# Cross attention and a mixture of experts: eight dense experts replaced by sorted blocks of the two chosen ones

## The chip, the cores and the metric

One Trainium2 chip, one of its cores. The metric is the device time of one execution of the whole kernel, in microseconds (us). The engines are TensorE (PE, with PEld its weight load), VectorE (DVE), ScalarE (ACT), GpSimd (POOL) and SyncE (SP, which only issues transfers here). Each runs its own instructions in order and waits on counting semaphores for the others.

## What is computed

Everything is float32. `x` is 64 sequences of 128 rows of 256; `ctx` has 64 x 128 rows of 192. Cut to what matters:

```
q, (k, v) = layernorm(x) @ Wq, ctx @ Wkv             # 16 heads of 64
x = x + (softmax(q k^T / 8) v) @ Wproj + bproj
t = layernorm(x)                                     # 8192 rows of 256
p = softmax(t @ gate_w.T)                            # 8 experts
w, e = top_k(p, 2)
y = sum over the two chosen: w * silu(t @ expert_w[e].T + expert_b[e])
x = x + y @ combine_w.T
```

## The kernel before

**Precision.** A float32 operand of a product is split in a high part (`_hi`, written by ACT) and the rest (`_lo`, the source less the high part, written by DVE from the same PSUM bank; for two of them by POOL). A product is then three matmuls: hi*hi, hi*lo, lo*hi (`three`, `products`, L355 to L363).

**Tiling.** The unit is a *pair* of sequences, 256 rows, so there are 32 pairs. Inside a pair the loop goes over 8 *slots* `u`, one for each pair of heads. In slot `u` of pair `i` PE issues, in this order: `scores(i,u)` (6 matmuls of 256 columns in the one bank `s_ps`), `turn_probs(u-1)` (4 transposes), `queries_keys(u+2)` (11 matmuls of 256 columns), the general jobs marked mid, `project(u-2)` (6), `attend(u-1)` (6), the general jobs marked late. DVE takes the row maximum (`row_max`, L707, the first DVE instruction of a slot), the low parts, and the reciprocal of the sums (`inverse`, L713); ACT the four exponentials (L567) and the high parts; POOL multiplies the probabilities by the reciprocals (`normalise_probs`, L939), which `turn_probs` of the next slot waits for. The low part of those transposed probabilities goes through ACT and DVE before `attend`.

**General jobs.** A table written out by hand says in which slot each further piece of work is issued, and for which pair relative to `i`; the jobs rotate through three PSUM banks `gen_ps`, and a job waits until the bank's last job has been drained:

```python
JOBS = [
    (0, "mid", "combine", 0, -3),
    (0, "late", "expert", 3, -2),
    (1, "mid", "value", 2, 0),
    (1, "late", "expert", 4, -2),
    ...
    (7, "mid", "turn_mixed", 0, -2),
    (7, "late", "expert", 2, -1),
]
```

So each slot ends with one `expert` job: 6 matmuls of 512 columns, that is two experts on 128 rows, and a pair has 8 of them (all 8 experts on its 256 rows). All expert weights stay in SBUF, split (`wexp_s`).

**After an expert job.** DVE adds the bias out of PSUM (`expert_bias`, L741), ACT takes tanh (L592) and adds one (L596), POOL multiplies (`silu`, L946), multiplies by the routing weights (L957, L960) and adds to the sum (`mix`, L962, L966), all on 128x512. Routing weights (`route_top`, `route_weights`, DVE, slot 6 of the next pair) are zero for the six experts not chosen. `turn_mixed` and `combine` (4 transposes, 12 matmuls of 256 columns) follow once a pair; the result plus `x1` goes out. In the last slots, where there is no attention left, DVE does what POOL does elsewhere (L748, L757, L763).

The matmuls of a job, and POOL's part behind it (`c` is the job's number within 128 rows):

```python
                for a in range(2):
                    terms += three(x1T[par], wexp_s, lambda y: y[:, a, t * P:(t + 1) * P],
                                   lambda w: w[:, a, c * 512:(c + 1) * 512])
                return products(bank[:, :], terms)
...
                pool.tensor_tensor(weighted.rearrange("p (e c) -> p e c", e=2), src, w, ALU.mult).then_inc(mix_done, 1)
                pool.wait_ge(mix_done, nth(j, 8, k))
                pool.tensor_tensor(acc, acc, weighted, ALU.add).then_inc(mix_step, 1)
```

**Order of the program.** `steps` writes pairs -1 to 3 and the last ones out, and runs pairs 4 to 28 in a loop of two pairs (`Fori`, 13 rounds). Once a pair POOL also computes two reciprocal roots for the norms (`rsqrt`, L932 and L934; the one for the next pair's norm in slot 1, ahead of `normalise_probs` of that slot), and adds the projection bias (L973). SP has two loads and one store a pair.

Of the kernel before, what the change touches and what calls it, by code (L numbers as in the profile page):

```python
# [5 lines left out]
P = 128  # L6
F32 = mybir.dt.float32
F32R = mybir.dt.float32r
U32 = mybir.dt.uint32
ALU = mybir.AluOpType  # L10
ACT = mybir.ActivationFunctionType
AX_X = mybir.AxisListType.X

# [4 lines left out]
EPS = 1e-5  # L28

JOBS = [
    (0, "mid", "combine", 0, -3),
    (0, "late", "expert", 3, -2),
    (1, "mid", "value", 2, 0),
    (1, "late", "expert", 4, -2),
    (2, "mid", "value", 3, 0),
    (2, "late", "expert", 5, -2),
    (3, "mid", "turn_x1", 0, -1),
    (3, "late", "expert", 6, -2),  # L40
    (4, "mid", "gate", 0, -1),
    (4, "mid", "turn_x", 0, 1),
    (4, "late", "expert", 7, -2),
    (5, "mid", "turn_gate", 0, -1),
    (5, "mid", "value", 0, 1),
    (5, "late", "expert", 0, -1),
    (6, "mid", "value", 1, 1),
    (6, "late", "expert", 1, -1),
    (7, "mid", "turn_mixed", 0, -2),
    (7, "late", "expert", 2, -1),  # L50
]
BANKS = 3
PER_PAIR = {"expert": 8, "value": 4, "turn_x": 1, "turn_x1": 1, "gate": 1, "turn_gate": 1,
            "turn_mixed": 1, "combine": 1}


def plus(j, n):
    return j + n if n else j


def nth(j, per, k):

    return plus(j * per if per != 1 else j, k + 1)


def exists(j, pairs):
    return not isinstance(j, int) or 0 <= j < pairs


def wait(eng, sem, count):  # L70

    if not isinstance(count, int) or count > 0:
        eng.wait_ge(sem, count)


def steps(eng, pairs, step):


    for i in (-1, 0, 1, 2, 3):
        step(i, i % 2)  # L80
    with eng.Fori(4, pairs - 3, 2) as i:
        step(i, 0)
        step(i + 1, 1)
    for i in (pairs - 2, pairs - 1, pairs, pairs + 1, pairs + 2):
        step(i, i % 2)


def xattn_moe_kernel(nc, x, ctxT, wq, wkv, wkv_rest, wproj, bproj, gateT, expertT, expert_b, combineT, out):
# [4 lines left out]
    N2 = 2 * P  # L93

    x_pairs = x.rearrange("(j t p) c -> j p t c", t=2, p=P)
    out_pairs = out.rearrange("(j t p) c -> j p t c", t=2, p=P)

    with ExitStack() as stack:
# [9 lines left out]

# [4 lines left out]
        wexp_s = hilo("wexp_s", [P, 2, E * C])  # L113
# [3 lines left out]
        ebias = sb("ebias", [P, E * C])  # L117
        pbias = sb("pbias", [P, C])
        ident = sb("ident", [P, P])
        minus_half = sb("minus_half", [P, 2])  # L120
        eps = sb("eps", [P, 2])
        expert_no = sb("expert_no", [P, E])

# [4 lines left out]


# [3 lines left out]

# [89 lines left out]
        def bank_free(pe, i, n):  # L223

            m = n
            while True:
# [7 lines left out]
                if isinstance(i, int) and i - step_back < -1:  # L234
                    return

        def tail_no(j, k):

# [807 lines left out]
```

## Time and profile before

| | |
|---|---|
| time, 3 runs | 1789.58 us median (1788.9 to 1792.51) |
| span of the profiled execution | 1787.3 us (its own time beyond the span is not listed; the median is 2.3 us above it) |
| first and last slot's row maximum | 29.5 us, 1726.5 us |
| PE busy | 1665.2 us (93%) |
| DVE busy | 1541.9 us (86%) |
| ACT busy | 1385.2 us (78%) |
| POOL busy | 1256.7 us (70%) |
| bytes moved by DMA | 42.89 MB |
| granted TensorE clock | 1.00 up to 1700 us, then 0.89, 0.84 and 0.80 in the three last stretches of some 30 us |

Times count from the start of the span. Busy times of an engine are merged, so overlapping instructions count once; a matmul's own duration contains its latency, and the distance between the starts of two of them is what one costs. The distance between two row maxima is the length of a slot.

### The profile page before, as it was taken

The page shows a single profiled execution, that of the slowest core. Times are in us where ns is not written, and L with a number is a line of the kernel's source. Part 1 is how long each engine was busy: PE and PEld are TensorE (multiplying, and loading weights), DVE is VectorE, ACT ScalarE, POOL GpSimd, SP SyncE. Part 2 cuts the span into 40 slices and gives each one's busy share as a digit, 9 for nine tenths or more (in the row PEclk, how much of TensorE's full clock was granted, in tenths as well). Part 3 has the DMA queues.
Part 4 walks back from the last instruction along what each step waited for, and adds up shares of the span by engine and source line. Part 5 has one row for each costly group of instructions (what it writes and reads, how often), then busy time and mean ns, then how long its engine had stood idle before and what let it go on. Part 6 is the DMA issues. An engine that isn't in the chain of part 4 may idle for free.

```text
span 1787.3 us, 39425 instructions
## 1 busy us (share of the span) xinstructions
PE 1665.2 (93%) x11584; PEld 1529.9 (86%) x11584; DVE 1541.9 (86%) x3569; ACT 1385.2 (78%) x4484; POOL 1256.7 (70%) x1235
## 2 busy tenths in 40 slices
PE   5999999999999999999999999999999999999986
PEld 4899889888888888888888898888898888888974
DVE  6888988888988888888888988889888888988877
ACT  6987878777878778788787887778787787887862
POOL 3557777777777777777776777777777777777760
PEclk9999999999999999999999999999999999999997
DMA  5000000000000000000000000000000000000000
GB/s 197 25 19 19 19 25 25 16 22 19 18 24 25 12 25 18 18 24 24 13 24 13 24 24 25 12 19 18 24 25 12 25 18 19 24 24 13 13 7 12
DMA packets 33609, 42.89 MB, mean 24 GB/s; under 512 B 2464, under 2 KB 28448, under 8 KB 32800
## 3 DMA queue, kind: packets, MB, share of 16 engines
q1 hardware_dynamic: 33440, 41.30, 7.2%
q14 instruction: 145, 1.19, 0.2%
q8 instruction: 24, 0.39, 0.1%
HBM read 32.91 MB, written 8.39 MB: 23 GB/s over the span
## 4 chain that ended last, share of the span: by engine, by line
PE 68%; DVE 16%; issue 12%; ACT 3%; DMA 1%; DVEq 1%; POOL 0%; SPq 0%; ACTq 0%; POOLq 0%
PE gen_ps L357 26%; PE qk_ps L357 11%; PE proj_ps L357 9%; PE o_ps L357 8%; PE s_ps L357 8%; DVE o_s_lo L675 4%; PE pT_ps L396 4%; DVE k_s_lo L675 2%; ACT probs L567 1%; DVE scratch L695 1%; DVE scratch L741 1%; DVE neg_max L707 1%; PE gen_ps L439 1%; DVE v_s_lo L675 1%; DVE top_atf L802 1%
## 5 line engine op out<-in xcount | busy, mean ns | idle before, releaser
L939 POOL TENSOR_TENSOR probs<-probs,inv_sums 128x512 f32<-128x512 f32 x256 | 268.8, 1050 | 275.6 <-DVE inv_sums L713 273.6
L946 POOL TENSOR_TENSOR scratch<-scratch 128x512 f32<-128x512 f32 x244 | 313.7, 1286 | 129.5 <-ACT scratch L596 129.5
L567 ACT ACTIVATE probs<-s_ps,neg_max 128x128 f32<-128x128 f32 x1024 | 363.2, 372 | 48.7 <-DVE neg_max L707 47.1
L552 ACT CAST pT_s_hi<-pT_ps 128x512 fp32r<-128x512 f32 x256 | 150.5, 588 | 223.6 <-PE pT_ps L396 220.7
L707 DVE TENSOR_REDUCE neg_max<-s_ps 128x4 f32<-128x512 f32 x256 | 175.9, 687 | 130.0 <-PE s_ps L357 100.7
L962 POOL TENSOR_TENSOR scratch<-scratch 128x512 f32<-128x512 f32 x183 | 236.8, 1294 | 14.3
L592 ACT ACTIVATE scratch<-scratch 128x512 f32<-128x512 f32 x256 | 161.9, 633 | 84.4 <-DVE scratch L741 79.2
L675 DVE TENSOR_TENSOR o_s_lo<-o_ps,o_s_hi 64x256 fp32r<-64x256 f32 x512 | 213.5, 417 | 5.6 <-ACT o_s_hi L552 1.9
L675 DVE TENSOR_TENSOR k_s_lo<-qk_ps,k_s_hi 64x256 fp32r<-64x256 f32 x512 | 213.3, 417 | 3.5
L567 ACT ACTIVATION_READ_ACCUMULATOR probs<-s_ps,neg_max 128x1 f32 x1024 | 215.7, 211 | 0.0
L357 PE MATMUL gen_ps<-wexp_s_hi,x1T_hi 128*128 128x512 f32 x512 | 205.5, 401 | 3.5 <-DVE scratch L741 3.4
L960 POOL TENSOR_TENSOR scratch<-scratch,route_w 128x512 f32<-128x512 f32 x183 | 190.4, 1040 | 26.0 <-POOL scratch L946 21.8
L357 PE MATMUL gen_ps<-wexp_s_lo,x1T_hi 128*128 128x512 f32 x512 | 204.5, 399 | 0.0
L357 PE MATMUL gen_ps<-wexp_s_hi,x1T_lo 128*128 128x512 f32 x512 | 203.4, 397 | 0.0
L552 ACT CAST k_s_hi<-qk_ps 64x256 fp32r<-64x256 f32 x512 | 190.9, 373 | 3.0
L552 ACT CAST o_s_hi<-o_ps 64x256 fp32r<-64x256 f32 x512 | 185.1, 361 | 5.3 <-PE o_ps L357 1.3
L357 PE MATMUL o_ps<-pT_s_hi,v_s_hi 128*128 128x256 f32 x512 | 148.1, 289 | 37.7 <-DVE pT_s_lo L675 37.7
L675 DVE TENSOR_TENSOR pT_s_lo<-pT_ps,pT_s_hi 128x512 fp32r<-128x512 f32 x256 | 176.8, 691 | 6.5
L357 PE MATMUL proj_ps<-wproj_s_hi,o_s_hi 128*128 128x256 f32 x512 | 155.3, 303 | 27.7 <-DVE o_s_lo L675 26.1
L741 DVE TENSOR_TENSOR scratch<-gen_ps,ebias 128x512 f32<-128x512 f32 x256 | 174.4, 681 | 3.1 <-PE gen_ps L357 3.0
L357 PE MATMUL qk_ps<-xT_hi,wq_s_hi 128*128 128x256 f32 x512 | 166.0, 324 | 3.9 <-DVE k_s_lo L675 3.8
L596 ACT ACTIVATE scratch<-scratch 128x512 f32<-128x512 f32 x244 | 154.8, 635 | 1.1
(134 smaller groups left out, 5640.3 us busy)
## 6 DMA issues: line engine op xcount, KB each, us to landing
x_raw<-in_x SPq DMA_DIRECT2D x32, 256.0 KB, 2.9
c_raw<-in_ctxT SPq DMA_DIRECT2D x32, 256.0 KB, 2.7
later<-in_x SPq DMA_DIRECT2D x32, 256.0 KB, 2.7
out_dram<-later SPq DMA_DIRECT2D x32, 256.0 KB, 2.2
scratch<-in_expertT SPq DMA_DIRECT2D x2, 1024.0 KB, 6.7
scratch<-in_wq SPq DMA_DIRECT2D x1, 1024.0 KB, 7.3
scratch<-in_wkv SPq DMA_DIRECT2D x1, 1024.0 KB, 9.3
ebias<-in_wkv_rest SPq DMA_DIRECT2D x1, 1024.0 KB, 11.4
```

The source lines that it names most:

```text
L357: mm = pe.matmul(out_ap, l, r, start=start and n == 0, stop=stop and n == len(terms) - 1, skip_group_check=skip)
L552: last = act.copy(to, of)
L567: last = act.activation(probs[p % 2][:, k, :], s_ps[:, k * P:(k + 1) * P], ACT.Exp, bias=neg_max[p % 2][:, k:k + 1], accum_out=sums[p % 2] ...
L592: act.activation(th[k % 2], z[k % 2], ACT.Tanh, scale=0.5).then_inc(tanh_done, 1)
L596: act.activation(th[k % 2], th[k % 2], ACT.Copy, bias=1.0).then_inc(tanh_plus, 1)
L675: last = dve.tensor_tensor(lo, of, hi.bitcast(F32), ALU.subtract)
L707: dve.tensor_reduce(neg_max[p % 2][:, :], s_ps[:, :].rearrange("p (k n) -> p k n", k=4), AX_X, ALU.max, negate=True).then_inc(max_done, 1)
L741: dve.tensor_tensor(z[k % 2], gen_ps[b][:, :], ebias[:, c * 512:(c + 1) * 512], ALU.add).then_inc(drained["expert"], 1)
L939: pool.tensor_tensor(probs[b][:, :, :], probs[b][:, :, :], inv_sums[b][:, :].unsqueeze(2).broadcast_to([P, 4, P]), ALU.mult).then_inc(prob ...
L946: pool.tensor_tensor(th[k % 2], th[k % 2], z[k % 2], ALU.mult).then_inc(silu_done, 1)
L960: pool.tensor_tensor(weighted.rearrange("p (e c) -> p e c", e=2), src, w, ALU.mult).then_inc(mix_done, 1)
L962: pool.tensor_tensor(acc, acc, weighted, ALU.add).then_inc(mix_step, 1)
```

## The change

The eight dense experts go. Each row is computed for its two experts only:

* **Routing** (DVE, PE): the two chosen experts of a row become a 0/1 mark (`hot`); one small PE job (`rank`, slot 7 of the next pair) counts how many earlier rows chose the same expert, and `route_rows` turns that into row numbers of a DRAM table `sorted_x`, which has a region for each expert.
* **Scatter** (POOL): in slot 0, two pairs later, 4 indirect transfers of 128 rows each write the normalised rows to `sorted_x`.
* **Chunks:** the 32 pairs are cut in chunks of 10, 9, 8 and 5. At a chunk's end `list_blocks` (DVE, some 25 small instructions) rounds each expert's count up to 128 and lists the blocks; `clear` (POOL, 8 indirect transfers) fills the rest of the last blocks with zeros. A chunk has 4n+7 blocks: 47, 43, 39 and 27, or 156.
* **Blocks:** one a slot. SP reads row and expert number from SBUF into a register and loads 128 rows (128 KB), the expert's split weights out of a DRAM table (512 KB) and its bias. PE transposes the rows (2 transposes), multiplies (6 matmuls of 256 columns and one for the bias); ACT and DVE split the rows and do tanh and (tanh+1)*z on 128x256; SP stores the block to `sorted_y`. The buffers form a ring of three.
* **Gather** (POOL): once a chunk's blocks are stored, each of its pairs takes two slots: 4 indirect transfers fetch the rows (128 KB each), POOL multiplies by the weights (128x1024) and adds (128x512), then `turn_mixed` and `combine` as before. `x1` of each pair is stored to DRAM and loaded back.
* **Program:** written out in full, with no loop. By the plan, chunk 0's blocks are turned in slots 92 to 138, chunk 1's in 164 to 206, chunk 2's in 228 to 266, chunk 3's in 268 to 294; gathers are at every second slot from 143, 211, 271 and 299. Attention ends with slot 255, the program with slot 313.

The core of the diff:

```diff
-JOBS = [
...
-def steps(eng, pairs, step):
...
+CHUNKS = (10, 9, 8, 5)
+RING = 3
...
+        for c, end in enumerate(self.ends):
+            at = max(at, SLOTS * (end + 1) + 4)
+            for b in range(self.blocks[c]):
+                self.turn[at] = (c, b, self.first[c] + b)
+                at += 1
+            free = max(free, at + 4)
+            for m in range(end - CHUNKS[c], end):
+                self.gather[free] = m
+                free += 2
...
+            def load_block(c, b, n):
...
+                if b == 0:
+                    sp.wait_ge(cleared, 16 * E * (c + 1))
...
+                wait(sp, made["turn_block"], n - RING + 1)
+                row = sp.value_load(blocks[b:b + 1, c, 0:1], min_val=0, max_val=ROWS - P)
+                sp.dma_start(x_block[r], sorted_x[bass.ds(row, P), :]).then_inc(x_block_in[r], 16)
+                wait(sp, made["expert"], n - RING + 1)
+                e = sp.value_load(blocks[b:b + 1, c, 1:2], min_val=0, max_val=E)
+                sp.dma_start(w_block[r][:, :, :].bitcast(F32).rearrange("p a n -> p (a n)"),
+                             expert_table[bass.ds(e * P, P), :]).then_inc(w_block_in[r], 16)
+                sp.dma_start(b_block[r][0:2, :].bitcast(F32),
+                             bias_table[bass.ds(e * 2, 2), :]).then_inc(b_block_in[r], 16)
+
+            def store_block(c, b, n):
+                sp.wait_ge(drained["expert"], n + 1)
+                sp.dma_start(sorted_y[c][b * P:(b + 1) * P, :], y_block[n % RING]).then_inc(y_stored[n % RING], 16)
...
+                if s - 2 in plan.turn:
+                    store_block(*plan.turn[s - 2])
+                if s + 2 in plan.turn:
+                    load_block(*plan.turn[s + 2])
...
+            def expert(n, bank):
+                pe.wait_ge(drained["turn_block"], n + 1)
+                pe.wait_ge(w_block_in[n % RING], 16 * (n // RING + 1))
...
+                for a in range(2):
+                    terms += three(xs, (w[:, a, :], w[:, 2 + a, :]), lambda y: y[:, a, :], lambda part: part)
+                terms.append((ones_s[:, :], b_block[n % RING][:, :]))
+                return products(bank[:, 0:C], terms)
...
+            def expert_out(n):
+                dve.wait_ge(tanh_done, n + 1)
+                wait(dve, y_stored[n % RING], 16 * (n // RING))
+                bank = gen_ps[plan.bank("expert", n)]
+                dve.scalar_tensor_tensor(out=y_block[n % RING], in0=th[n % 2], scalar=1.0, in1=bank[:, 0:C],
+                                         op0=ALU.add, op1=ALU.mult).then_inc(drained["expert"], 1)
...
+            def scatter(j):
+                pool.wait_ge(xn2_done, j + 1)
+                pool.wait_ge(rows_done, j + 1)
+                for k in range(4):
+                    pool.indirect_dma_start(
+                        out=sorted_x, out_offset=bass.IndirectOffsetOnAxis(ap=row_of[:, j % 4, k:k + 1], axis=0),
+                        in_=xn2[j % 2][:, k // 2, :], in_offset=None).then_inc(scattered[j % 2], 16)
+
+            def clear(c):
+                pool.wait_ge(clear_ready, c + 1)
+                pool.wait_ge(zero_ready, 1)
+                wait(pool, cleared, 16 * E * c)
+                for e in range(E):
+                    pool.indirect_dma_start(
+                        out=sorted_x, out_offset=bass.IndirectOffsetOnAxis(ap=clear_at[:, c, e:e + 1], axis=0),
+                        in_=zero_rows[:, :], in_offset=None).then_inc(cleared, 16)
+
+            def gather(m):
...
+                for r in range(RING):
+                    pool.wait_ge(y_stored[r], 16 * blocks_in_ring(r, through))
+                pool.wait_ge(y_rows_done, c + 1)
+                wait(pool, mixed_done, m - 1)
+                for k in range(4):
+                    pool.indirect_dma_start(
+                        out=got[m % 2][:, k, :], out_offset=None, in_=sorted_y[c],
+                        in_offset=bass.IndirectOffsetOnAxis(ap=y_row_of[:, m, k:k + 1], axis=0)).then_inc(
+                            gathered[m % 2], 16)
+
+            def mix(m):
+                pool.wait_ge(gathered[m % 2], 64 * (m // 2 + 1))
+                pool.wait_ge(top_w_done, m + 1)
+                y = got[m % 2]
+                pool.tensor_tensor(y, y, top_w[:, m, :].unsqueeze(2).broadcast_to([P, 4, C]),
+                                   ALU.mult).then_inc(weighted, 1)
+                pool.wait_ge(weighted, m + 1)
+                wait(pool, made["turn_mixed"], m - 1)
+                pool.tensor_tensor(mixed[m % 2], y[:, 0:4:2, :], y[:, 1:4:2, :], ALU.add).then_inc(mixed_done, 1)
...
+            for s, i, u in slots():
+                now, before, nxt = exists(i), exists(i - 1), exists(i + 1)
+                if u == 1 and nxt:
+                    rsqrt(i + 1, 0)
+                if now:
+                    normalise_probs(i, u)
+                if u == 2 and before:
+                    rsqrt(i - 1, 1)
+                if s - 2 in plan.gather:
+                    mix(plan.gather[s - 2])
+                if s in plan.gather:
+                    gather(plan.gather[s])
+                if u == 0 and exists(i - 2):
+                    scatter(i - 2)
+                    if i - 1 in plan.ends:
+                        clear(plan.ends.index(i - 1))
```

## Rows read from the trace of the kernel before

**Rows 1.** The page, busy time of each engine.

```profile
PE 1665.2 (93%) x11584; PEld 1529.9 (86%) x11584; DVE 1541.9 (86%) x3569; ACT 1385.2 (78%) x4484; POOL 1256.7 (70%) x1235
```

**Rows 2.** The page, chain that ended last, shares of the span by engine.

```profile
PE 68%; DVE 16%; issue 12%; ACT 3%; DMA 1%; DVEq 1%; POOL 0%; SPq 0%; ACTq 0%; POOLq 0%
```

**Rows 3.** Windows: length, busy time (x count) of each engine, clock, DMA share, GB/s.

```profile
68.00:95.00 27.00, 25.92 (x198) 23.91 (x197) 24.88 (x61) 22.54 (x78) 10.29 (x12) 1.00 0.10 31
```

**Rows 4.** Timeline, DVE row maxima: start, duration, idle before and releaser.

```profile
29.48 0.69 DVE L707 TENSOR_REDUCE neg_max<-s_ps 128x4 f32<-128x512 f32 x1
...
68.22 0.69 DVE L707 TENSOR_REDUCE neg_max<-s_ps 128x4 f32<-128x512 f32 x1
...
112.45 0.69 DVE L707 TENSOR_REDUCE neg_max<-s_ps 128x4 f32<-128x512 f32 x1 [0.86 <-PE s_ps L357]
...
164.27 0.69 DVE L707 TENSOR_REDUCE neg_max<-s_ps 128x4 f32<-128x512 f32 x1 [0.36 <-PE s_ps L357]
...
217.43 0.69 DVE L707 TENSOR_REDUCE neg_max<-s_ps 128x4 f32<-128x512 f32 x1 [0.46 <-PE s_ps L357]
...
976.78 0.69 DVE L707 TENSOR_REDUCE neg_max<-s_ps 128x4 f32<-128x512 f32 x1 [2.38 <-issue]
...
1726.47 0.69 DVE L707 TENSOR_REDUCE neg_max<-s_ps 128x4 f32<-128x512 f32 x1 [2.27 <-PE s_ps L357]
```

**Rows 5.** Timeline, PE: starts of neighbouring matmuls and four transposes.

```profile
1000.37 0.28 PE L357 MATMUL s_ps<-k_s_hi,q_s_hi 128*128 128x256 f32 x1
...
1000.49 0.28 PE L357 MATMUL s_ps<-k_s_lo,q_s_hi 128*128 128x256 f32 x1
...
1005.18 0.39 PE L357 MATMUL gen_ps<-wexp_s_hi,x1T_hi 128*128 128x512 f32 x1
...
1005.41 0.39 PE L357 MATMUL gen_ps<-wexp_s_lo,x1T_hi 128*128 128x512 f32 x1
```

**Rows 6.** Groups by line and shape: count, busy us, mean ns, idle before.

```profile
L946 POOL TENSOR_TENSOR scratch<-scratch 128x512 f32<-128x512 f32 x244 | 313.7, 1286 | 129.5 <-ACT scratch L596 129.5
L939 POOL TENSOR_TENSOR probs<-probs,inv_sums 128x512 f32<-128x512 f32 x256 | 268.8, 1050 | 275.6 <-DVE inv_sums L713 273.6
...
L741 DVE TENSOR_TENSOR scratch<-gen_ps,ebias 128x512 f32<-128x512 f32 x256 | 174.4, 681 | 3.1 <-PE gen_ps L357 3.0
...
L675 DVE TENSOR_TENSOR q_s_lo<-qk_ps,q_s_hi 128x256 fp32r<-128x256 f32 x256 | 104.5, 408 | 44.4 <-ACT k_s_hi L552 44.4
...
L934 POOL TENSOR_TENSOR rstd<-var_eps,minus_half 128x2 f32<-128x2 f32 x64 | 44.8, 700 | 5.0
...
L819 DVE TENSOR_TENSOR route_w<-chosen 128x16 f32<-128x16 f32 x32 | 35.9, 1121 | 3.4
...
L1010 POOL TENSOR_SCALAR_AFFINE_SELECT ident<-ident 128x128 f32<-128x128 f32 x1 | 0.3, 292 | 0.2 <-POOL ident L1008 0.2
```

**Rows 7.** Timeline of pair 1, POOL multiplications and the transposes after one.

```profile
71.48 1.04 POOL L939 TENSOR_TENSOR probs<-probs,inv_sums 128x512 f32<-128x512 f32 x1 [1.65 <-DVE inv_sums L713]
...
75.61 1.04 POOL L939 TENSOR_TENSOR probs<-probs,inv_sums 128x512 f32<-128x512 f32 x1 [0.26 <-DVE inv_sums L713]
...
77.68 0.60 PE L396 MATMUL pT_ps<-ident,probs 128*128 128x128 f32 x4
```

**Rows 8.** Timeline of SP: start and length of an issue.

```profile
1.76 0.43 SPq L321 DMA_DIRECT2D scratch<-in_wq  x1
...
3.69 5.76 SPq L327 DMA_DIRECT2D gate_raw<-in_gateT  x1
```

**Rows 9.** DMA issues: count, KB each, median us from issue to landing.

```profile
x_raw<-in_x SPq DMA_DIRECT2D x32, 256.0 KB, 2.9
...
out_dram<-later SPq DMA_DIRECT2D x32, 256.0 KB, 2.2
```

**Rows 10.** Timeline, DVE: gate logits of the last pair.

```profile
1753.42 0.25 DVE L779 TENSOR_REDUCE logits<-gen_ps 128x8 f32<-128x16 f32 x2
```

**Rows 11.** The chain that ended last, its last transposes.

```profile
1778.20 1.10 PE gen_ps L439 x4
```

More of the change, by code:

```diff
@@ L28 @@
 EPS = 1e-5
-JOBS = [
[L33 to L51, printed above, removed]
@@ L52 @@
-BANKS = 3
[L53 to L67, printed above, removed]
+ROUND = 8388608.0
+CHUNKS = (10, 9, 8, 5)
+RING = 3
+BANKS = 3
+ATTENTION_JOBS = {
+    1: [("value", 2, 0)],
+    2: [("value", 3, 0)],
+    3: [("turn_x1", 0, -1)],
+    4: [("gate", 0, -1), ("turn_x", 0, 1)],
+    5: [("turn_gate", 0, -1), ("value", 0, 1)],
+    6: [("value", 1, 1)],
+    7: [("rank", 0, -1)],
+}
@@ L353, in _ @@
+                if s - 5 in plan.gather:
+                    m = plan.gather[s - 5]
+                    sp.wait_ge(drained["combine"], m + 1)
+                    sp.dma_start(out_pairs[m], outb[m % 2].rearrange("p (t c) -> p t c", t=2)).then_inc(
+                        out_stored[m % 2], 16)
+            for b in range(2):
+                sp.wait_ge(out_stored[b], 16 * (pairs // 2))
         @block.tensor
@@ L504, in general @@
                     else:
[L505 removed]
+                        mm = combine(n, bank)
                     mm.then_inc(made[kind], 1)
[L508 to L532 removed]
@@ L534, in _ @@
-            steps(pe, pairs, step)
-        def previous_expert(i, u, back=1):
-            for slot, _, kind, k, off in JOBS:
-                if kind == "expert" and slot == (u - back) % SLOTS:
-                    off -= u < back
-                    if exists(plus(i, off), pairs):
-                        return k, plus(i, off), off
-            return None
+            pe.wait_ge(const_b, 2)
+            for s, i, u in slots():
+                now, before, nxt = exists(i), exists(i - 1), exists(i + 1)
+                if now:
+                    scores(i, u)
+                if u == 0 and before:
+                    turn_probs(i - 1, 7)
+                if u > 0 and now:
+                    turn_probs(i, u - 1)
+                if u < 6 and now:
+                    queries_keys(i, u + 2)
+                if u >= 6 and nxt:
+                    queries_keys(i + 1, u - 6)
+                general(s, "mid")
+                if u < 2 and before:
+                    project(i - 1, 6 + u)
+                if u >= 2 and now:
+                    project(i, u - 2)
+                if u == 0 and before:
+                    attend(i - 1, 7)
+                if u > 0 and now:
+                    attend(i, u - 1)
+                general(s, "late")
```

1132 lines of the change are left out of this document (622 added, 510 removed).

## The prediction, made before any run of the changed kernel

> **What bounds the kernel now.** I read the page's busy line first: PE 93%, DVE 86%, ACT 78%, POOL 70% [rows 1]. Two engines are near full, so the chain that ended last decides between them: 68% of it is PE and 16% DVE [rows 2]. The issue share, 12%, has to be found elsewhere: it sits at the loop.
>
> Then the starts of the row maxima, one a slot [rows 4]. They cut the span in a start (29.5 us), 255 slots (1697 us) and an end of 61 us. Pair 3 takes 217.43 - 164.27 = 53.2 us. Pair 1 is a natural experiment: its slots 0 to 4 have no expert at all, only three expert jobs fall in it, and it takes 112.45 - 68.22 = 44.2 us. In its window without experts PE is busy 25.9 of 27 us and DVE 24.9 [rows 3], so attention alone keeps both nearly full. POOL is not: 10.3 us.
>
> **What an expert job costs today.** Let A be a pair without experts and e one job. Pair 1 is A + 3e. Pair 3 is A + 8e + 3.4, where 3.4 is 1.9 for `turn_mixed` and `combine` (16 PE instructions at about 0.12, the distance of two starts [rows 5]) and an estimate of 1.5 for DVE instructions that take longer beside POOL (the group of 16 elements that averages 1121 ns [rows 6] is the plainest). So 53.2 - 3.4 - 44.2 = 5e: e = 1.1, A = 40.9. A job costs 6 x 0.23 = 1.4 us of PE [rows 5] and 0.68 of DVE [rows 6]; a fifth of the PE time is hidden.
>
> **Removed.** 8e a pair; the three POOL instructions of 128x512 a job; all tanh work on 512 columns; the loop. At a back edge DVE's row maximum shows 2.38 us of issue idle [rows 4]; with 12 back edges, and about a half given back in the next slot, that is 15 to 28 us. The sum below has it, since it is built from unrolled pairs.
>
> **Added, attention part (slots 0 to 255).**
> - Routing: `rank`, five row instructions, two `hot`: some 8 DVE instructions of 0.13 us (two in 0.25 [rows 10]). 1.1 us a pair, so a pair is 42.0.
> - Base: 29.5 + 32 x 42.0 - 3 (pair 0 took 38.7, 68.22 - 29.48) - 5 (the last slot's own length) = 1366.
> - Blocks: 118 of the 156 fall in attention slots. One is 7 x 0.12 + 2 transposes of 0.12, 1.1 us of PE, and two DVE instructions of 128x256, 0.41 each [rows 6]. By PE's ratio to a dense job that is 0.85 us of slot, by DVE's 1.3; unhidden, 1.9. I take 0.85, since PE holds the chain: 100. Their ACT work (two instructions of 256 columns) replaces two of 512.
> - 19 pairs combined here: 19 x 1.9 = 36. Three block lists of some 25 linked small instructions, 0.2 each: 15.
>
> Without the indirect transfers slot 255 would start at 1517, 210 us earlier than today.
>
> **The indirect transfers** decide. POOL must write the descriptors of 128 rows; the trace of before has none. Call one c. From below: a small POOL instruction, 0.29 [rows 6]. From above: SP's issue of the gate weights, many small pieces, 5.76 us, against 0.43 for a plain one [rows 8]. Nearest in kind are POOL instructions that go over 128 rows: 1.05 and 1.29 [rows 6]. I take 1.1.
>
> What is late next: `normalise_probs` of the following slot stands behind them on POOL, `turn_probs` on PE waits for it, and all of PE's slot stands behind that. In pair 1 two of these POOL instructions start 4.13 us apart (slots 0 and 1), and after the second `turn_probs` starts 77.68 - 76.65 = 1.0 us after its end [rows 7]; that is the slack.
> - Scatter in slot 0: 4c = 4.4, plus `rsqrt` 0.9 (0.70 [rows 6] and a smaller one) and the multiplication 1.05, is 6.35. Late by 2.2, less 1.0 slack: 1.2 x 30 pairs = 36.
> - Clear, 8c = 8.8 behind a scatter, three times in attention: 26.
> - A gather slot has mix of the pair before (2 x 1.05 + 1.29 = 3.4), 4.4 and 1.05, 8.85 us, against a slot of 5.3 and 1.0 slack: 2.5 x 19 = 48.
>
> Slot 255 then starts at 1366 + 100 + 36 + 15 + 36 + 26 + 48 = 1627.
>
> **The tail, from there.** Attention's last pair needs 26.9 us to its gate logits today [rows 4, 10], and about 2 more to its row numbers: 29. Scatter to 33.4, meanwhile the list to about 34, clear 8.8, landing 2.2 (a store [rows 9]): 45. SP then reads the row number and loads, 2.9 [rows 9], turned and multiplied at about 50. Eleven blocks of chunk 2 fit in before. Chunk 3's 27 blocks go at about 3 us each (four SP issues of 0.43 [rows 8], two register reads that no row shows, a round trip of DVE between). POOL in that time gathers 8 pairs, and each is 4.4, 2.2 landing, 3.4 mix, one after the other since mix precedes the next gather: 10.0, so from 45 to 125, longer than PE's 19 blocks (107); seven more blocks, 146; last out and stored, 150. Then five pairs at 10.0 with nothing beside them, 200. The end, from the turned mix to the end of the span, is 1787.3 - 1778.2 = 9.1 today [rows 11]. Tail: 209 us, against 61.
>
> Sum: 1627 + 209 = **1836 us**, against the span of 1787.3. The median stands 2.3 above its span; I write 1836, as the sum is not that fine. The expert work saved is given back once in POOL's queue and once in a tail.
>
> **A rule weighed.** The row of 16 elements with a mean of 1121 ns [rows 6] shows DVE held up while POOL works. The Trainium skill, "SBUF — State Buffer", Who interferes with whom, says the two share a port pair by an exclusive lock, and that descriptor generation on GpSimd is shut out while DVE copies in its two-port mode: the first half helps this change (by that, DVE gets its 1.5 us a pair back, which the sum has), the second speaks against it and is rival 2. The skill's "DMA: Bandwidth & Descriptors", Anatomy of one DMA, gives about 2.0 us fixed for a transfer issued from GpSimd, mostly completion; with that for the landing the sum would be some 3 us less.
>
> **Rivals.**
> 1. Descriptors are cheap, c = 0.7 or less (nearer to a small POOL instruction). Then scatter hides (4.75 against 5.13), clear costs 16, gathers 16, slot 255 starts at 1549, the tail is 185: 1734 us, faster. It decides below c = 0.92, where scatter costs 12, clear 21, gathers 31 and the tail about 197. For: POOL is idle 17 of 27 us in pair 1. Against: no POOL instruction over 128 rows is below 1.05. Chance 0.26.
> 2. A descriptor waits for DVE: with one DVE instruction of 0.4 [rows 6] in front of each transfer, c = 1.5: 85 + 36 + 77 and a tail of 233: 1948. For: DVE is busy 24.9 of 27 us, though few of its instructions are copies. Chance 0.14.
> 3. SP becomes the bound: registers and four issues at over 5 us a block. In attention hidden by the slot; in the tail 38 blocks at 5 instead of 3, less what POOL's pace covers: 1880 to 1900. Chance 0.10.
> 4. Blocks hide nothing: 1.9 instead of 0.85 on 118, 1960. Against: dense jobs hid a fifth. Chance 0.04.
> The forecast, c between 0.92 and 1.4: 0.46, with 1790 to 1920 as its own range.
>
> **Chances and range.** Within 0.2% of 1789.6 is about what a measurement can tell from no change; the forecast's low edge and rival 1's upper edge meet there: 0.03. Faster 0.26, slower 0.71. Range: down to 1734 for rival 1, up to 1950 for rivals 2 and 3.
>
> **What would show it.** The profile after should have: PE near 75 to 80% busy and POOL's queue issue rows of about 1.1 us in fours; `turn_probs` waiting for POOL in slots 1 and in gather slots, hundreds of waits of 1 to 3 us; pairs without blocks and gathers (3 to 9) of 43 us; 7 us more for each pair with a block in every slot; the last row maximum at about 1627; some 200 us after it with PE mostly idle, and in the last 50 only POOL's gathers and mixes. Wrong would make it: c off 1.1 by a few tenths, each 0.1 being about 26 us; blocks at another price than 0.85; a wait for `w_block` or for SP that I don't see.

## The result and the profile after

The changed kernel takes 2006.9 us (median of 4 runs, 2004.5 to 2011.6) where the one before takes 1790.7 us in the same comparison: ratio 1.1215, 95% interval 1.1197 to 1.1232. It is slower, as I forecast, but by 216 us where I had 46, and 57 us above the top of my range. The profiled execution's span is 2009.8 us.

The page after, busy time; it answers to [rows 1]:

```profile
PE 1596.0 (79%) x11516; PEld 1471.5 (73%) x11516; DVE 1436.0 (71%) x3879; ACT 1202.7 (60%) x4298; POOL 795.4 (40%) x865
```

Every engine has less to do than before, and none is full. So this is a kernel that waits, and the view to read is the chain's local form, the waits. (The chain that ended last has only 4% of the span attributed here, and says nothing.) Who waited for whom: total, times, longest.

```profile
POOL probs L1087 <- DVE inv_sums L821: 991.2, 209, 9.9
ACT pT_s_hi L637 <- PE pT_ps L481: 385.6, 244, 12.1
DVE stage L844 <- ACT stage L694: 180.4, 148, 1.8
PEld pT_ps L481 <- POOL probs L1087: 139.2, 102, 11.0
```

POOL's 991 us cost nothing by themselves: it has little to do, and waits for its next job. The third row is the one that I had not priced. `expert_out` (L844), DVE's last instruction on a block, waits 148 times, 1.2 us each, for ACT's tanh (L694), and DVE is an engine on which all else stands behind it.

Two stretches show the size. The row maxima (L814), one a slot, as in [rows 4]; first those of a pair without blocks (its start, the two ends of its slot 2, the next pair's start), then those of a pair with a block in every slot (its start, its slots 2 to 4, the next pair's start):

```profile
382.39 0.69 DVE L814 TENSOR_REDUCE neg_max<-s_ps 128x4 f32<-128x512 f32 x1
...
392.10 0.68 DVE L814 TENSOR_REDUCE neg_max<-s_ps 128x4 f32<-128x512 f32 x1
399.16 0.68 DVE L814 TENSOR_REDUCE neg_max<-s_ps 128x4 f32<-128x512 f32 x1
...
426.95 0.69 DVE L814 TENSOR_REDUCE neg_max<-s_ps 128x4 f32<-128x512 f32 x1
...
699.66 0.68 DVE L814 TENSOR_REDUCE neg_max<-s_ps 128x4 f32<-128x512 f32 x1
...
712.29 0.68 DVE L814 TENSOR_REDUCE neg_max<-s_ps 128x4 f32<-128x512 f32 x1
720.26 0.68 DVE L814 TENSOR_REDUCE neg_max<-s_ps 128x4 f32<-128x512 f32 x1
728.26 0.68 DVE L814 TENSOR_REDUCE neg_max<-s_ps 128x4 f32<-128x512 f32 x1
...
757.71 0.68 DVE L814 TENSOR_REDUCE neg_max<-s_ps 128x4 f32<-128x512 f32 x1
```

The pair with blocks takes 757.71 - 699.66 = 58.05 us. The one without takes 426.95 - 382.39 = 44.56 (the slot shown, 7.06 us, has the scatter stall in it). The difference is 13.5 us over eight blocks: **1.69 us a block**, where I had 0.85. And here is why, in the slot from 720.26: ACT, DVE, POOL and PE in order of time.

```profile
720.98 0.37 ACT L665 ACTIVATE probs<-s_ps,neg_max 128x128 f32<-128x128 f32 x1 [0.38 <-DVE neg_max L814]
...
722.36 0.63 ACT L657 CAST cT_hi<-c_raw 128x512 fp32r<-128x512 f32 x1
722.38 0.69 DVE L772 TENSOR_TENSOR pT_s_lo<-pT_ps,pT_s_hi 128x512 fp32r<-128x512 f32 x1
722.87 0.39 ACT L637 CAST q_s_hi<-qk_ps 128x256 fp32r<-128x256 f32 x1
723.14 0.76 ACT L637 CAST k_s_hi<-qk_ps 64x256 fp32r<-64x256 f32 x2
723.92 0.38 ACT L694 ACTIVATE stage<-gen_ps 128x256 f32<-128x256 f32 x1
...
724.34 0.42 DVE L844 SCALAR_TENSOR_TENSOR stage<-stage,gen_ps 128x256 f32<-128x256 f32 x1 [1.26 <-ACT stage L694]
...
724.67 0.17 DVE L821 RECIPROCAL inv_sums<-sums 128x4 f32<-128x4 f32 x1
724.81 0.50 PE L444 MATMUL gen_ps<-w_block,xbT_hi 128*128 128x256 f32 x2 [0.70 <-DVE stage L844]
724.92 1.12 POOL L1087 TENSOR_TENSOR probs<-probs,inv_sums 128x512 f32<-128x512 f32 x1 [4.79 <-DVE inv_sums L821]
```

The softmax sums are there when ACT's last exponential ends, near 722.5. DVE could take the reciprocal (L821) at 723.1, when the low part of pT is done. It does so at 724.67, because `expert_out` stands ahead of it and waits for a tanh that ACT has placed behind the exponentials and the high parts of q and k.

Three things stand behind that wait. One is the reciprocal, with POOL's multiplication and PE's `turn_probs` after it. One is the rest of DVE's slot: from 724.34 to the next row maximum at 728.26 DVE is never idle, so the 1.26 us are in the slot's length. And one is a PSUM bank: `expert_out` is also what empties it, and PE waits 0.70 us for that (724.81) ahead of the next block's matmuls, with the next slot's scores behind them. `turn_probs` then goes at 726.46, right behind those scores and 0.4 us after POOL has finished.

Over the three pairs from 699.66 to 873.83 us, DVE is idle 12.7 us a pair, 10.9 of them at `expert_out`. PE waits 5.3 us a pair for the bank that `expert_out` empties, and 2.2 us for POOL's probabilities; in the pairs without blocks that last wait is 2.1 us. So what the late tanh adds on PE is the wait for the bank, and not the path over the reciprocal.

An indirect transfer, the other open price, is nearly uniform. POOL in the tail: four gathers of a pair and its multiplication and addition, first beside the blocks of the last chunk, then (second group) with nothing beside them:

```profile
1835.80 0.98 POOL L1124 DMA_INDIRECT stage<-sorted_y,y_row_of  x1 [0.15 <-POOL stage L1137]
...
1840.48 0.95 POOL L1124 DMA_INDIRECT stage<-sorted_y,y_row_of  x1 [0.31 <-issue]
1846.08 1.89 POOL L1133 TENSOR_TENSOR stage<-stage,top_w 128x1024 f32<-128x1024 f32 x1 [4.65 <-DMA stage<-sorted_y,y_row_of]
1848.05 1.26 POOL L1137 TENSOR_TENSOR stage<-stage 128x512 f32<-128x512 f32 x1
1849.46 0.98 POOL L1124 DMA_INDIRECT stage<-sorted_y,y_row_of  x1
...
1963.56 0.95 POOL L1124 DMA_INDIRECT stage<-sorted_y,y_row_of  x1 [0.30 <-issue]
1964.81 0.94 POOL L1124 DMA_INDIRECT stage<-sorted_y,y_row_of  x1 [0.30 <-issue]
1967.63 1.89 POOL L1133 TENSOR_TENSOR stage<-stage,top_w 128x1024 f32<-128x1024 f32 x1 [1.87 <-DMA stage<-sorted_y,y_row_of]
```

0.95 us and 0.30 between two: c = 1.26 from start to start, where I had 1.1. Beside blocks the gathered rows land 4.65 us after the last issue's end and a pair takes up to 13.7 us (1849.46 - 1835.80); alone, 1.87 us, and a pair takes 9.96 (mean of the last four steps).

### The profile page after: what moved, and what is told of

Its sections match the earlier page's. It is cut to its first block and busy times, and to the rows that moved or that the text cites. A ratio compares the mean times of both kernels' runs of the same rounds, so it can differ in the third digit from the quotient of the medians.

```text
span 2009.8 us, 39286 instructions
## 1 busy us (share of the span) xinstructions
PE 1596.0 (79%) x11516; PEld 1471.5 (73%) x11516; DVE 1436.0 (71%) x3879; ACT 1202.7 (60%) x4298; POOL 795.4 (40%) x865
## 5 line engine op out<-in xcount | busy, mean ns | idle before, releaser
L481 PE MATMUL pT_ps<-ident,probs 128*128 128x128 f32 x1024 | 162.9, 283 | 118.5 <-POOL probs L1087 118.2
L814 DVE TENSOR_REDUCE neg_max<-s_ps 128x4 f32<-128x512 f32 x256 | 175.2, 684 | 60.8 <-PE s_ps L444 60.2
L481 PEld LDWEIGHTS pT_ps<-ident,probs 128*128 128x128 f32 x1024 | 116.5, 143 | 139.2 <-POOL probs L1087 139.2
L844 DVE SCALAR_TENSOR_TENSOR stage<-stage,gen_ps 128x256 f32<-128x256 f32 x156 | 65.6, 421 | 180.4 <-ACT stage L694 180.4
L444 PE MATMUL proj_ps<-wproj_s_hi,o_s_hi 128*128 128x256 f32 x512 | 165.2, 323 | 33.2 <-DVE o_s_lo L772 31.0
L444 PE MATMUL gen_ps<-w_block,xbT_hi 128*128 128x256 f32 x624 | 145.9, 328 | 28.0 <-DVE stage L844 22.5
L1124 POOL DMA_INDIRECT stage<-sorted_y,y_row_of x128 | 123.9, 968 | 75.4 <-issue 71.3
L444 PE MATMUL o_ps<-pT_s_hi,v_s_lo 128*128 128x256 f32 x512 | 147.4, 288 | 0.0
L444 PE MATMUL o_ps<-pT_s_lo,v_s_hi 128*128 128x256 f32 x512 | 147.3, 288 | 0.0
L444 PE MATMUL s_ps<-k_s_hi,q_s_hi 128*128 128x256 f32 x512 | 146.4, 286 | 0.8 <-ACT probs L665 0.8
L1103 POOL DMA_INDIRECT sorted_x<-xn,row_of x128 | 126.4, 987 | 51.4 <-issue 34.3
```

The costliest lines, as they stand in the source:

```text
L444: mm = pe.matmul(out_ap, l, r, start=start and n == 0, stop=stop and n == len(terms) - 1, skip_group_check=skip)
L481: mm = pe.transpose(pT_ps[:, k * P:(k + 1) * P], probs[p % 2][:, k, :], ident[:, :])
L814: dve.tensor_reduce(neg_max[p % 2][:, :], s_ps[:, :].rearrange("p (k n) -> p k n", k=4), AX_X, ALU.max, negate=True).then_inc(max_done, 1)
L844: dve.scalar_tensor_tensor(out=y_block[n % RING], in0=th[n % 2], scalar=1.0, in1=bank[:, 0:C], op0=ALU.add, op1=ALU.mult).then_inc(drained ...
L1103: pool.indirect_dma_start(out=sorted_x, out_offset=bass.IndirectOffsetOnAxis(ap=row_of[:, j % 4, k:k + 1], axis=0), in_=xn2[j % 2][:, k // ...
L1124: pool.indirect_dma_start(out=got[m % 2][:, k, :], out_offset=None, in_=sorted_y[c], in_offset=bass.IndirectOffsetOnAxis(ap=y_row_of[:, m, ...
```

## The experiments

Ten kernels, in three groups (the first four, the next four, the last two), each with its own runs of the kernel before on the same chip: 1789.5, 1782.8 and 1785.8 us. All ratios are to those; between groups the ratios are what compares, and spans of the traces within one percent.

**The loop by itself.** The dense kernel with its loop written out, all else as before:

```diff
-    for i in (-1, 0, 1, 2, 3):
-        step(i, i % 2)
-    with eng.Fori(4, pairs - 3, 2) as i:
-        step(i, 0)
-        step(i + 1, 1)
-    for i in (pairs - 2, pairs - 1, pairs, pairs + 1, pairs + 2):
+    for i in range(-1, pairs + 3):
         step(i, i % 2)
```

> The dense kernel with its loop over pairs written out, nothing else changed. If the back edges cost what the trace of before shows (the pairs inside the loop take 52.1 and 56.2 us in turn, 54.15 on average, the written-out ones 53.1), 26 pairs save about 1.05 us each: 1790 - 27 = 1763 us. If the written-out program pays for fetching instructions instead, no change or slower.

Measured: 1762.4 us, ratio 0.9844 (0.9827 to 0.9860). The loop cost 27 us, inside my 15 to 28. So one part of the change is a gain, and the sparse part alone costs 245 us, not 216.

**Who holds the block slots.** Two kernels part the two orders. In the first, DVE's `expert_out` goes behind the reciprocal and the low parts of q and k, so that nothing in the softmax waits for tanh:

```diff
-                if s - 2 in plan.turn:
-                    expert_out(plan.turn[s - 2][2])
...
                 if u >= 6 and nxt:
                     qk(i + 1, u - 6)
+                if s - 2 in plan.turn:
+                    expert_out(plan.turn[s - 2][2])
```

> The changed kernel; DVE issues expert_out after inverse and after the low parts of q and k, instead of before inverse. Theory A (DVE waits for a tanh that ACT runs behind the high parts of q and k, 1.2 us a block, and holds up inverse and so the loop over the probabilities): a slot with a block falls from 7.26 us to about 6.4, 118 slots, so some 100 us less, about 1905. Theory B (the three PSUM banks: the next block's transposes wait for expert_out): the later issue makes it longer, 2007 to 2060. Theory C (PE or DVE full): same.

In the second, ACT does the tanh of a block ahead of the exponentials; DVE's order is unchanged:

```diff
+                if s - 2 in plan.turn:
+                    tanh(plan.turn[s - 2][2])
                 if now:
                     exps(i, u)
...
-                if s - 2 in plan.turn:
-                    tanh(plan.turn[s - 2][2])
```

> The changed kernel; ACT issues the block's tanh before the exponentials of the slot, instead of behind the high parts of q and k. Theory A: DVE's wait goes, the exponentials start 0.3 us later; 118 slots save 0.6 to 0.9 us: 1900 to 1935. Theory B: the bank is free earlier too, so this gains more than the late expert_out: below 1905. Theory C: same.

The first was slower than the changed kernel itself: 2044.1 us, ratio 1.1412 (1.1378 to 1.1446). Its block pairs take 59.5 to 62.5 us. Waits for the bank, first of the whole changed kernel, then of this one:

```profile
PE gen_ps L552 <- DVE stage L844: 48.8, 26, 2.5
...
PE gen_ps L444 <- DVE stage L844: 22.5, 31, 1.0
```

```profile
PEld gen_ps L444 <- DVE stage L844: 101.4, 73, 2.3
...
PE gen_ps L444 <- DVE stage L844: 86.5, 72, 2.1
```

`expert_out` frees the PSUM bank of the block, and PE, in order too, stands before the next job that wants that bank. In its pairs from 703.40 to 886.92 us the reciprocal comes 2.9 us after the row maximum on average, as in a pair without blocks, and PE never waits for POOL's probabilities; but it waits 10.2 us a pair for the bank, where the changed kernel has 5.3. An early reciprocal alone gains nothing.

The second was far faster: 1896.5 us, ratio 1.0598 (1.0581 to 1.0616), 110 us off the changed kernel. Its block pairs take 50.74 us against 44.56: **0.77 us a block**. Two neighbouring pair starts, then a stretch of a slot in its trace (slot 7 of its pair; the one shown above was slot 3):

```profile
681.81 0.68 DVE L814 TENSOR_REDUCE neg_max<-s_ps 128x4 f32<-128x512 f32 x1
...
732.55 0.68 DVE L814 TENSOR_REDUCE neg_max<-s_ps 128x4 f32<-128x512 f32 x1
```

```profile
676.76 0.39 ACT L694 ACTIVATE stage<-gen_ps 128x256 f32<-128x256 f32 x1
...
677.03 0.37 ACT L665 ACTIVATE probs<-s_ps,neg_max 128x128 f32<-128x128 f32 x1
...
677.64 0.69 DVE L772 TENSOR_TENSOR pT_s_lo<-pT_ps,pT_s_hi 128x512 fp32r<-128x512 f32 x1
...
678.25 0.41 DVE L844 SCALAR_TENSOR_TENSOR stage<-stage,gen_ps 128x256 f32<-128x256 f32 x1
...
678.58 0.18 DVE L821 RECIPROCAL inv_sums<-sums 128x4 f32<-128x4 f32 x1
678.84 1.04 POOL L1087 TENSOR_TENSOR probs<-probs,inv_sums 128x512 f32<-128x512 f32 x1 [4.16 <-DVE inv_sums L821]
```

`expert_out` follows the low part of pT with no wait, and the reciprocal comes 2.4 us after the slot's row maximum (676.17), where the changed kernel's slot 7 has 3.9. In such pairs DVE is idle 4.7 us instead of 12.7, and PE waits 1.0 us for the bank instead of 5.3. The block's own work is cheap, and was priced right; the place of one ACT instruction doubled it. Both times fell where my expectations had put theory B, the bank (2007 to 2060, and below 1905): theory A, the reciprocal, had the first at 1905.

**The scatter.** One transfer in each of the slots 0 to 3 instead of four in slot 0 (at a chunk's end still all four):

```diff
-                if u == 0 and exists(i - 2):
+                if u < 4 and exists(i - 2) and i - 1 not in plan.ends:
+                    scatter(i - 2, (u,))
+                if u == 0 and i - 1 in plan.ends:
                     scatter(i - 2)
...
```

> The changed kernel; a pair's four scatter transfers are issued one each in slots 0 to 3 instead of all in slot 0 (not in the four steps in which a clear follows). If the 1.6 us by which slot 2's start is late (7.06 against 5.48 us) is POOL's queue: 26 pairs x 1.6 = 42 us less, 1965. If it were the transfers themselves (SBUF or DMA), no change.

Measured: 1981.2 us, ratio 1.1077 (1.1058 to 1.1095), 26 us off, where I expected 42. Pairs without blocks fall from 44.56 to 43.22. Most block pairs stay at 57.9 to 58.2: the slot that held the scatter stall takes 7.05 us instead of 7.98, but two slots later one takes 9.0 instead of 8.07. Why it gives the gain back was not traced.

**The gather's order on POOL.** The gather of a pair ahead of the mix of the pair before:

```diff
-                if s - 2 in plan.gather:
-                    mix(plan.gather[s - 2])
                 if s in plan.gather:
                     gather(plan.gather[s])
+                if s - 2 in plan.gather:
+                    mix(plan.gather[s - 2])
```

> The changed kernel; in a slot POOL issues the next pair's four gathers ahead of the mix of the pair before. In the tail one pair takes POOL 12.5 us beside block loads (four transfers 5.1, landing 4 to 5 waited out, mix 3.3) and 10.0 without. Theory: the landing is waited out only because mix stands right behind the transfers; swapped, a pair is 8.4 us, so the last five pairs save 5 x 1.6 = 8 us, and the eight before them save 8 x 4 = 32 us of POOL, of which some is then PE's or SP's block pace: 1975 to 1990. Rival: the tail goes at the pace of the blocks, not of POOL: only the 8 us, 2000. In the attention part no change (the mix comes two slots later).

A miss: I expected 1975 to 1990, and no change in attention. In the tail it does what was meant (a pair every 8.8 us; the tail is 216 us instead of 245), but the kernel took 2024.8 us, ratio 1.1365 (1.1348 to 1.1383), where the changed kernel has 1.1215. The last row maximum comes at 1803.0 instead of 1765.2: the gather pairs in attention rise from 57.5 and 65.3 us to 65.3 and 75.9. Waits of its pairs with gathers, 1000 to 1080 us:

```profile
PE gen_ps L524 <- POOL stage L1137: 13.7, 4, 4.0
```

The mix now comes 5 us later in its slot, and PE's `turn_mixed`, which stands ahead of attention's own work, waits 4.0 us for it. In that stretch of the changed kernel this row is absent; PE waits there for POOL's `probs` instead (16.6 us in 4 waits).

**The weights.** The experts' weights and biases are loaded for the first three blocks only and those are used for all (that part of the computation is left out, and PE waits for those first loads only):

```diff
             def load_block(c, b, n):
...
+                if n >= RING:
+                    return
```

> The changed kernel with the expert weights and biases of a block loaded for the first three blocks only; every later block is multiplied by whatever the ring holds, so the output is of other experts. It takes 153 x 514 KB of loads and SP's second wait away and leaves all else. Theory: in the attention part the loads cost nothing (each has some three slots), so the block pairs stay at 58.0 us; in the tail the landing of a gather falls from 4.5 to 2 us, so POOL's cycle falls from 12.5 to 10 and the tail by 20 to 30 us: 1980. Rival: SP's queue and the loads are part of the block slots' length: block pairs shorter, 1900 to 1950.

Measured: 1983.4 us, ratio 1.1123 (1.1106 to 1.1140); the span is 1983.2 us, against 2009.8. The last row maximum is at 1765.9, as with the loads: 512 KB a block cost attention nothing. The tail is 217 us instead of 245. Windows over the tail's first part, of the changed kernel, then of this one (length, busy time and count of PE, PEld, DVE, ACT, POOL, clock, DMA share, GB/s):

```profile
1800.00:1930.00 130.00, 65.65 (x351) 61.15 (x352) 31.41 (x66) 23.20 (x58) 63.90 (x57) 0.70 0.73 226
```

```profile
1800.00:1900.00 100.00, 54.37 (x302) 50.90 (x303) 26.93 (x56) 20.25 (x50) 58.02 (x52) 0.74 0.48 142
```

**All of it spread.** Tanh first, the scatter spread, the clear two transfers a slot over slots 0 to 3 (the first three chunks' blocks then start two slots later):

> The changed kernel with the tanh before the exponentials, one scatter transfer a slot, and the clears of the first three chunks two a slot over slots 0 to 3 (their blocks start two slots later); not the last chunk's. From 1896 for the tanh alone: 26 for the scatter as measured, and the three clears cost 10.8 us each in slot 2: with three transfers a slot, 3.8 us, they fit into POOL's idle 3.3 to 4.7 us and the 1.0 us of slack, so 25 to 32 less: about 1840. If the clears' cost is SP held at its wait for them, it stays: 1870.

```diff
-                if u == 0 and exists(i - 2):
-                    scatter(i - 2)
+                if i - 1 == pairs:
+                    if u == 0:
+                        scatter(i - 2)
+                        clear(len(CHUNKS) - 1)
+                elif u < 4 and exists(i - 2):
+                    scatter(i - 2, (u,))
                     if i - 1 in plan.ends:
-                        clear(plan.ends.index(i - 1))
+                        clear(plan.ends.index(i - 1), (2 * u, 2 * u + 1))
```

Measured: 1861.5 us, ratio 1.0439 (1.0419 to 1.0459), where I expected 1840; block pairs 50.15 us. The first pair with a clear takes 46.5 us instead of 60.6, but two of its block slots have moved to the next pair as well; its slots 0 to 3, ahead of any block's matmuls, take 24.0 us instead of 34.7. Then the same with each pair's four gathers two a slot over two slots, the multiplication in the third and the addition in the fourth, `turn_mixed` and `combine` a slot later:

```diff
+                if s in plan.gather:
+                    gather(plan.gather[s], (0, 1))
+                if s - 1 in plan.gather:
+                    gather(plan.gather[s - 1], (2, 3))
                 if s - 2 in plan.gather:
                     mix(plan.gather[s - 2])
-                if s in plan.gather:
-                    gather(plan.gather[s])
...
+                if s - 3 in plan.gather:
+                    add_two(plan.gather[s - 3])
```

> As the run before, and the gathers spread too: two transfers a slot over two slots, the multiplication in the third, the addition in the fourth, gathers ahead of them; turn_mixed and combine one slot later. In the attention part a gather costs 3.2 to 3.7 us now, of which 1.9 is PE's own work: 19 x 1.5 = 28 less. In the tail POOL's pair falls from 12.5 and 10.0 to 8.4: 40 less. From 1840: about 1775, 14 under the dense kernel. Rival: the tail is at the blocks' pace: 1800.

Measured: 1811.0 us, ratio 1.0157 (1.0143 to 1.0171), the last row maximum at 1594.4 and a tail of 217 us. I expected 1775: attention gave 20 us instead of 28, the tail 27 instead of 40. The first pair full of gathers takes 49.0 us, where the run before has 56.0, and the next 60.3 instead of 63.9 (5.1 of each a block list); in that next pair PE's wait for POOL's probabilities is down from 9.9 to 0.9 us, so the slots hardly queue on POOL any more.

**Against the tail.** The last kernel with chunks of 12, 10, 6 and 4 pairs, so that less is left at the end:

```diff
-CHUNKS = (10, 9, 8, 5)
+CHUNKS = (12, 10, 6, 4)
```

> The kernel with tanh first and all indirect transfers spread, with its chunks changed from 10, 9, 8 and 5 pairs to 12, 10, 6 and 4, so that the last chunk has 23 blocks instead of 27 and 10 gathered pairs fall behind the last row maximum instead of 13. Theory that the tail is set by the stored blocks of the last chunk (they were waited for until about 164 us behind the last row maximum): 36 blocks instead of 40 in the tail at 4.1 us each end 16 us earlier, and 4 pairs of 8.7 us follow instead of 5: the tail falls from 217 to about 192 us. The attention part takes 4 more blocks at 0.77 and 3 more gathered pairs at about 2 us, so +9: near 1795 us, level with the dense kernel (ratio 1.00). Rival, that GpSimd's mixing of the earlier chunk sets the tail and the blocks wait on nothing: 3 pairs fewer at 8.7, which the attention part gives back in part: 1790 to 1800 too, but with GpSimd not idle ahead of the last chunk's gathers. If the blocks are bound by their loads beside the gathers, the tail falls by less than 10 us and the kernel stays near 1810.

And the same with the tail's additions on DVE:

```diff
+                if s - 3 in plan.gather and s > SLOTS * (pairs + 1):
...
+                    dve.tensor_tensor(mixed[m % 2], y[:, 0:4:2, :], y[:, 1:4:2, :], ALU.add).then_inc(mixed_done, 1)
```

> The same chunks of 12, 10, 6 and 4, and behind the last row maximum the addition of the two weighted rows goes from GpSimd to VectorE. If GpSimd's cycle of four transfers, a product and an addition (8.7 us) sets the end, it falls to about 7.2 us, and the four last pairs end 6 us earlier: about 1789 us. If the stored blocks set the end, only those four pairs gain, and the middle of the tail stays: the same 6 us. If VectorE in order holds the addition behind a block's output, nothing is gained or up to 10 us lost.

Measured: 1801.8 us, ratio 1.0091 (1.0076 to 1.0107), and 1800.2 us, ratio 1.0089 (1.0075 to 1.0103). Both gains are smaller than expected (1795 and 1789), the second nothing that can be told. With fewer blocks left (36 instead of 40), the last chunk's gathers still start 165 us after the last row maximum (164 in the kernel before it). Its waits and the window over 1680 to 1720 show why:

```profile
ACT xbT_hi L637 <- PE gen_ps L552: 20.1, 9, 4.3
PE gen_ps L552 <- DMA stage<-sorted_x: 13.6, 7, 4.0
...
1680.00:1720.00 40.00, 26.09 (x142) 23.93 (x142) 13.20 (x27) 9.92 (x24) 31.64 (x27) 0.66 0.93 298
```

PE's transposes of a block wait for its rows, up to 4.0 us, with the DMA engines 93% busy at 298 GB/s. That looks like the third outcome that I had written down for this run, blocks bound by their loads. But SP, which issues these loads, hardly waits either: 0.9 us in these 40. It issues the rows of ten blocks there, and over the last chunk never two of them less than 3.26 us apart; each block is four issues of some 0.3 us and two register reads. PE takes up a block's rows 3.0 to 5.9 us after their issue, where it is 8 to 17 us in attention. So SP is late with the loads, and its queue bounds the blocks at least as much as their landing does. No run parts the two: the one without weight loads takes both away (its rows' loads come down to 1.58 us apart).

With DVE's addition in the tail, something else shows. Three of POOL's gather transfers that start 0.12 us after such an addition take 1.42 or 1.43 us:

```profile
1765.43 0.69 DVE L1028 TENSOR_TENSOR stage<-stage 128x512 f32<-128x512 f32 x1 [11.79 <-POOL stage L1139]
...
1765.55 1.42 POOL L1130 DMA_INDIRECT stage<-sorted_y,y_row_of  x1 [0.16 <-issue]
```

Two that were under way before an addition began took 0.96 and 0.98.

## Why the prediction was wrong, by its own steps

The span is 174 us above my sum: 138 of it by the last row maximum (1765.2 against 1627), 36 behind it (244.6 against 209).

| term | predicted | measured | difference |
|---|---|---|---|
| pair without blocks | 42.0 | 43.0 | x32: +32 |
| block, a slot | 0.85 | 1.69 | x118: +99 |
| scatter stall | 1.2 | 1.58 | x30: +11 |
| clear, three | 26 | 32 | +6 |
| combine and gather, a pair | 1.9 + 2.5 | 3.2 to 3.9 | x19: -16 |
| three lists | 15 | 15 | 0 |
| start, end, rest | | | +6 |
| tail | 209 | 244.6 | +36 |

(1.58: slot 2 of a quiet pair takes 7.06 in the changed kernel, 5.48 with the scatter spread, whose slot 3 gives 0.24 back; 43.0 is 44.56 less 1.58. Clear: the first one's slot takes 17.83 instead of 7.06, 10.8 more; the three are put at that. Gather pairs: 57.48 and, less a list of 5.1, 60.2 against 44.56, by four pairs each. In block pairs, spreading the scatter gave nothing back, so there the split between its stall and the block is only the table's.)

**The step that failed: "I take 0.85, since PE holds the chain."** The work was sized right: with tanh first it is 0.77. What the step left out is what my own text asks elsewhere: where the change adds a wait, what is queued behind the waiting instruction? I counted `expert_out` as 0.41 us of DVE. It also waits, 1.2 us each of 148 times, for an ACT instruction that stands behind four exponentials and the high parts of q and k. Behind it, in order, stand the reciprocal and the rest of DVE's slot, and PE's next job stands before the bank that it empties. The order to see this was in the code before any run: ACT's tanh behind `exps` in its slot, DVE's `expert_out` ahead of the reciprocal, and three banks in turn for all of PE's general jobs. Moving ACT's instruction took 110 us out of the kernel, and 118 blocks at 1.69 - 0.77 are 109; moving DVE's took nothing out and added 37 us, with PE's waits for the bank doubled. The share of each of the three followers in the 1.69 is not told apart, beyond what PE's waits say: the bank's is there, the reciprocal's is not. Without the 99 us by which this one term was mis-sized the time would have come out at 1908, inside my range. The 1.69 is near rival 4 in size (1.9, "hides nothing"), to which I gave 0.04, but not in mechanism: the block's work does hide.

**Pair without blocks.** A with its routing is 1.0 us dearer than by my decomposition of pairs 1 and 3, which rested on an estimate of 1.5 us for the sharing of DVE and POOL. Which part of it is off was not tried, and stays open.

**The indirect transfers.** c is 1.27 in the scatter (0.987 busy, 0.30 between) and 1.26 in the gather, inside the 0.92 to 1.4 on which the forecast rested. Rival 1 (0.7 or less) falls by it. Rival 2 falls too: in the changed kernel all 288 transfers last 0.94 to 1.22 us, half of them 0.96 or less, with DVE 75% busy beside them in block pairs, so they don't wait for DVE's instructions one by one. That is where the Trainium skill's "SBUF — State Buffer", Who interferes with whom, would have had longer ones if DVE's copies kept the descriptors out, and this trace doesn't show it. Not every DVE instruction is harmless, though: beside the additions of the last run, both of whose inputs lie in SBUF, three transfers took 1.42 us. The way in which the stalls arise was as written: spread over slots, the scatter costs 0.24 instead of 1.58, and slots 0 to 3 of the pair with the first clear are 10.7 us shorter.

Two terms beside rival 1 are added up wrongly: at c = 0.92 the scatter is 0.50 x 30 = 15 (not 12) and the gathers 1.83 x 19 = 35 (not 31). The forecast doesn't use them.

**The tail.** Right until the row numbers (30.3 us after the last row maximum against 29) and right where POOL is alone (9.96 us a pair against 10.0). Wrong between, by 13, 20 and 3 us. The first gather starts at 58 instead of 45; by the code it waits for chunk 2's last blocks to be stored. The eight pairs beside blocks take 12.6 us each instead of 10.0, since their rows land 3.9 to 5.0 us after the issue instead of 2.2. The last chunk's gathers then start 27.4 us later instead of 25, at 185.9 instead of 150. I took a landing time from a store with nothing beside it, and used it where 512 KB loads share the engines: without the weight loads, rows land 2.5 to 3.6 us after the issue, and the three numbers are 48, about 11.4 and 158.4. (That run takes two of SP's four issues of a block away too, so the 48 and the 158.4 are not the DMA's alone.)

That POOL's pairs set the pace there was forecast, and the waits agree: between 1823 and 1951 us PE waits 43.5 us for POOL's addition, ahead of `turn_mixed`, with blocks queued behind it, and 17.7 us for a block's rows. The kernel with the gather first changes no load, and its tail is 28 us shorter as well. Rival 3 named SP as the tail's bound. In the changed kernel SP waits 27 of the 102 us from 1823 to 1925, 23 of them for PE, so it was not; with the gathers spread it waits 5.5 of 102, and there rival 3 may hold, at 3.3 us a block and not its 5.

**The mechanism of the whole** stands as far as the tail goes. With the stalls in attention that I found taken away or made small, the sparse kernel takes 1800 us, 0.9% over the dense one and 2.5% over the dense one unrolled (1.0089 / 0.9844 = 1.0249). Against that unrolled one its last row maximum comes 108 us earlier (1591.3 against 1699.6), and what follows takes 145 us more (207.0 against 61.7): the tail alone gives back more than all of attention has gained. No sparse version here beats either.

## What to carry to other kernels

Price a new instruction by what it waits for and by what stands behind it on its engine, not by its length: here one 0.38 us tanh in the wrong place cost 110 us. Ask also what the waiting instruction frees: a later consumer left PE standing before its PSUM bank, and the cure was to issue the producer earlier. A change that makes work depend on data (sort, store, read back) bought a tail of 207 to 245 us here, with PE busy about half of it; ask what is left to run after the last of the old work, with transfer times taken beside the load that will be there and the issuing engine's own pace counted. And before a gain is put down to an algorithm, run the old one with the same loop form.

## What the runs showed of the hardware

- An indirect transfer of 128 rows costs POOL 0.94 to 1.22 us (medians 0.95 and 0.96), and 0.30 to the next of a row, for scatter, clear and gather alike.
- Started 0.12 us after a DVE addition of 128x512 with both inputs in SBUF, it took 1.42 or 1.43 us, three times of three; started before one, 0.96 and 0.98.
- Its landing depends on company: 1.87 us after the last issue alone, 3.9 to 5.0 beside 512 KB loads with the DMA engines 73% busy, and 2.5 to 3.6 in the same place without those loads (48% busy).
- A block's three loads and one store, with two values read into registers for them, keep SP for some 3.3 us: where it waits for nothing its loads of rows follow one another at 3.26 to 3.3 us (1.58 without the weight and bias loads and their read).
- PE's granted clock is lower where it waits more: 0.99 in attention's block pairs (641 to 873 us, PE busy 85%), 0.70 over 1800 to 1930 (busy 51%) and 0.60 over the last 79 us of the changed kernel, where PE is busy 30 of 79 us. The last two are mixes of its two levels, 2.4 and 1.2 GHz. What this costs in the tail was not measured by itself.
